# Small bf16 products on TensorE in and ahead of the router stages of a four-layer network

## The chip, the cores and the metric

The kernel runs on one core of a Trainium2 chip. The metric is the device time of one execution in microseconds (us); lower is better. TensorE's granted clock is given in the profile as a share of full speed: 1.00 is 2.4 GHz, 0.50 is 1.2 GHz.

## The reference, cut to what matters

Four layers, each an attention and then a feed-forward, over 8 x 256 = 2048 tokens of width 256. Two of the feed-forwards, those of layer 0 and of layer 3, route tokens to eight experts. The change touches only what stands at their start: the normalisation and the router's product.

```python
def _L0_ffn_ref(x, Wr, br, W_up, b_up, W_down, b_down):
    xf = x.reshape(n_tok, h)
    logits = xf @ Wr + br                     # 2048 x 256 by 256 x 8
    Sm = jax.nn.softmax(logits, axis=-1)
    G_t, idx_t = jax.lax.top_k(Sm.T, k)       # each expert takes its 256 best tokens
    ...
def _L3_ffn_ref(x, router_w, w1, w2):
    logits = x_flat @ router_w.T              # 2048 x 256 by 256 x 8
    probs = jax.nn.softmax(logits, axis=-1)
    top_v, top_i = jax.lax.top_k(probs, K)    # each token takes its 2 best experts
    ...
x = x + jnp.tanh(g_ffn[0]) * _L0_ffn_ref(_layernorm(x, axis=-1), ...)
...
x = x + jnp.tanh(g_ffn[3]) * _L3_ffn_ref(_layernorm(x, axis=-1), ...)
```

## The kernel before

Each engine has its own program, written out by hand; semaphores order them, and nothing reorders them. The stages follow each other: attention 0, feed-forward 0, attention 1, and so on. Tokens lie 128 to a tile on the partitions, in `X` (16 tiles); two tiles make a pair, so there are 8 pairs. The two feed-forwards named in `GATHERED` start like this:

- VectorE adds the last attention output to `X` (line 2238), takes the statistics (line 2014 and the short steps at lines 2020 to 2030), then normalises pair by pair into a ring of four tiles `xn` (line 2069). SyncE writes each normalised pair to memory (line 586), from where the experts' tokens are gathered later.
- TensorE waits for a pair, and turns it with four f32 transposes of 128x128 into one PSUM bank (`turn_normed`, line 828). ScalarE copies that bank to `XNT` (line 1581).
- TensorE multiplies the turned pair by the router's weights (`router`, line 836): four products a pair, each with 128 tokens as the stationary operand and the 8 columns of the router's weights as the moving one. In the profile each of these f32 products is two instructions, so a pair shows 8; a transpose is one.
- The order on TensorE is three turns, then router product and turn in alternation, and the router products of the last three pairs at the end (`layernorm`, from line 841).
- The last router product releases VectorE, which works out the softmax and the routing from the logits in `ps[0]` (from line 2477 in feed-forward 0, from line 2479 in feed-forward 3). In feed-forward 0 ten rounds of counting on VectorE and TensorE follow, in feed-forward 3 the building of slot lists; then come the experts.

The feed-forward of layer 2 uses `turn_normed` too, with no router; that of layer 1 uses it in bf16. `ident` is the f32 identity of 128x128, `ident_bf` the same in bf16. Line 1040 is the output product of an attention, the last that TensorE does before `layernorm`.

Of the kernel before, what the change touches and what calls it, by code (L numbers as in the profile page):

```python
# [8 lines left out]
BF16 = mybir.dt.bfloat16  # L9
# [66 lines left out]
LNB = 4  # L76
PAIRS = NT // ST
W2_PIECES = 4
FREE = 1
SENT0 = 16  # L80
QSTEPS = 6
# [3 lines left out]
def program(nc, a, out, stages):  # L85
    ctx = ExitStack()
    with ctx:
# [3 lines left out]
        def sb(name, shape, dt, c=ctx):  # L91
            return c.enter_context(nc.sbuf_tensor(name, shape, dt))
# [11 lines left out]
        ident = sb("ident", [P, P], F32)  # L104
        ident_bf = sb("ident_bf", [P, P], BF16)
# [194 lines left out]
        ps = [ctx.enter_context(nc.psum_tensor(f"ps{i}", [P, 2, S], F32)) for i in range(8)]  # L300
# [36 lines left out]
        GATHERED = (("ffn", 0), ("ffn", 3))  # L337
        g_order = {st: i for i, st in enumerate([st for st in stages if st in GATHERED])}

        def wait(eng, semaphore, value):  # L340

            if not isinstance(value, int) or value > 0:
                eng.wait_ge(semaphore, value)
# [55 lines left out]
        def ready_x(eng, n):  # L399

            kind, L = stages[n - 1]
            if kind == "att":
                eng.wait_ge(s["x_res"], FREE + 8 * (order["att", L] + 1))
            else:
# [21 lines left out]
        def keys_in(L, b):  # L426
            return ps[3] if L == 3 and b < 2 else P1
# [16 lines left out]
        def exists(b):  # L444
            return not isinstance(b, int) or 0 <= b < B
# [9 lines left out]
        def _(sp):  # L455
# [14 lines left out]
            def send_rows(n, b):  # L470

                rows = table[stages[n][1]]
                sp.wait_ge(s["x_res"], FREE + 8 * order["att", stages[n][1]] + b + 1)
                sp.dma_start(rows[b * S:(b + 1) * S].rearrange("(t p) c -> p t c", p=P), X[:, ST * b:ST * b + ST]).then_inc(s["rows_ready"], 16)
# [327 lines left out]
        def _(pe):  # L802
            pe.sem_inc(s["y_ps"], FREE)
            pe.wait_ge(s["ident_ready"], 3)
# [3 lines left out]
            def turn_pair(n, pair):  # L808
# [5 lines left out]
                        last = pe.transpose(turned_in(L, pair)[:, c, tt * P:(tt + 1) * P], normed_in(L, pair)[:, tt, c * P:(c + 1) * P], ident[:])  # L814
                last.then_inc(s["xnt_psum"], 1)

            def turn_normed(n, first, j):
                pair = PAIRS * n + first + j
                pe.wait_ge(s["xn_ready"], pair + 1)
                pe.wait_ge(s["xnt_done"], pair + 1)  # L820
                bank = ps[2 + j][:]
                if stages[n] == ("ffn", 1):
                    src, bank, eye = qn[j], bank.bitcast(BF16), ident_bf
                else:
                    src, eye = xn[j], ident
                for tt in range(ST):
                    for c in range(KC):
                        last = pe.transpose(bank[:, c, tt * P:(tt + 1) * P], src[:, tt, c * P:(c + 1) * P], eye[:])
                last.then_inc(s["xnt_psum"], 1)

            def router(n, pair, w):

                pe.wait_ge(s["xnt_done"], PAIRS * n + LNB + pair + 1)
                for t in range(ST * pair, ST * pair + ST):
                    for c in range(KC):
                        mm = pe.matmul(ps[0][:].rearrange("p a b -> p (a b)")[:, t * E0:(t + 1) * E0], XNT[:, c, t * P:(t + 1) * P],
                                       w[:, c], start=c == 0, stop=c == KC - 1)
                if pair == PAIRS - 1:
                    mm.then_inc(s["rt_logits"], 1)

            def layernorm(n):
                if stages[n] not in GATHERED:
                    with pe.Fori(0, PAIRS // LNB) as t:
                        for j in range(LNB):
                            turn_normed(n, LNB * t, j)
                    return

                L = stages[n][1]
                pe.wait_ge(s["rt_const"], 5)  # L850
                for pair in range(PAIRS):
                    turn_normed(n, pair - pair % LNB, pair % LNB)
                    if pair == 1:
                        pe.wait_ge(s["router"], 48 if L == 0 else 16 + 48 * (("ffn", 0) in stages))
                    if pair > 1:
                        router(n, pair - 2, wr0 if L == 0 else wr3)
                for pair in range(PAIRS - 2, PAIRS):
                    router(n, pair, wr0 if L == 0 else wr3)

            def projections(n, L):  # L860
# [4 lines left out]
                def key_product(b, par, v, f, c):  # L865
                    if (f, c) == (0, 0):
                        pe.wait_ge(ctx_sem[par], ctx_loads(i, par, v + 1))

                        if b < 4 or not keys:
                            wait(pe, k_read, 8 * i + b)  # L870
                            back = 5 if L == 1 else 4
                            if exists(b - back):
                                pe.wait_ge(s["x_res"], FREE + 8 * i + b - back + 1)
                        else:
                            pe.wait_ge(s["x_res"], FREE + 8 * i + b - 3)
                    mm = pe.matmul(keys_in(L, b)[:, f], wk[:, c, f * P:(f + 1) * P], ctxT[par][:, c], start=c == 0, stop=c == KC - 1)  # L876
# [30 lines left out]
            def attention(n, L):  # L907
# [100 lines left out]
                def output_turn(b):  # L1008
# [5 lines left out]
                    else:  # L1014
                        if exists(b + 1):
                            pe.wait_ge(s["m_lo"], 8 * m_order[L] + b + 2)
                        pe.wait_ge(s["x_res"], FREE + 8 * i + b)
                    for t in range(ST):
# [454 lines left out]
            def ffn3(n):  # L1473
# [34 lines left out]
                def down(b, k):  # L1508
# [3 lines left out]
                    for c in range(HT):  # L1512
                        if c % 2 == 0:
                            pe.wait_ge(s["f3_w2l"], W2_PIECES * t + c // 2 + 1)
                        for j, (m, w) in enumerate(((mh3, w2h_3), (mh3, w2l_3), (ml3, w2h_3))):
# [24 lines left out]
            for n, (kind, L) in enumerate(stages):  # L1540
                if kind == "att":
                    attention(n, L)
                else:
                    layernorm(n)
                    (ffn0, ffn1, ffn2, ffn3)[L](n)
# [3 lines left out]
        def _(act):  # L1549
# [252 lines left out]
            def ffn0(n):  # L1802
                route_exp(0)

                act.wait_ge(s["thr_step"], 1)
                def copy(e):
                    act.wait_ge(s["f0_xt"], e + 1)
                    wait(act, s["f0_up"], FT0 * (e - 1))
                    act.activation(xgT0[e % 2][:], ps[5][:], ACT.Copy).then_inc(s["f0_xgT"], 1)

                copy(0)
                for e in range(E0):
                    for f in range(FT0):
                        rows = P if f < FT0 - 1 else FL0
                        act.wait_ge(s["f0_up"], FT0 * e + f + 1)
                        if f == 0:
                            wait(act, s["f0_down"], e - 1)
                        act.activation(mid0[e % 2][0:rows, f], ps[f % 3][0:rows, 0], ACT.Silu,
                                       bias=bu0[0:rows, e // 2, f:f + 1]).then_inc(s["f0_mid"], 1)
                    if e + 1 < E0:  # L1820
                        copy(e + 1)
                split_k, _, middle_k, _ = splits(n + 1, 1)
                split_k(0, 0, 0)
                middle_k(0, 0)
# [86 lines left out]
            def ffn3(n):  # L1911
# [10 lines left out]
                def hidden(t, k):  # L1922
                    act.wait_ge(s["f3_up"], t + 1)
                    wait(act, s["f3_piece"], W2_PIECES * (t - 1))
                    for half in range(2):
# [5 lines left out]
                def high_w2(t):  # L1931
                    e = act.value_load(expert3_i[0:1, ds(t, 1)], min_val=0, max_val=E3 - 1)
                    act.wait_ge(s["f3_loaded"], e + 1)
                    for p in range(W2_PIECES):
                        wait(act, s["f3_piece"], W2_PIECES * (t - 1) + p + 1 if not isinstance(t, int) or t else 0)
                        act.activation(w2h_3[:, 2 * p:2 * p + 2], w2_3[:, ds(e, 1), 2 * p:2 * p + 2].squeeze(1), ACT.Copy).then_inc(s["f3_w2h"], 1)  # L1936
# [28 lines left out]
        def _(dve):  # L1965
# [591 lines left out]
            def ffn0(n):  # L2557
# [61 lines left out]
                for e in range(E0 - 3, E0):  # L2619
                    weigh(e)  # L2620
                rest_k, _, low_k, _ = rests(1)
                rest_k(0, 0)
                low_k(0, 0)
# [131 lines left out]
            def route3(n):  # L2755
# [25 lines left out]
                for j in range(2):  # L2781
                    e = dve.tensor_tensor(row_m[:, j], row_m[:, 3 + j], row_m[:, 5], ALU.mult)
                chain(e)
                running_counts(2 * E3, lambda _, e: chain(e), 0, r)
                for j in range(PAIRS3):
                    of = slice(j * E3, (j + 1) * E3)
# [50 lines left out]
            def ffn3(n):  # L2837
# [16 lines left out]
                def weigh(t, k):  # L2854
                    dve.wait_ge(s["f3_piece"], W2_PIECES * (t + 1))
                    wait(dve, s["f3_scatter"], 16 * (t - 1))
                    dve.tensor_scalar(yg3[k % 2][:], ps[5 + 2 * (k % 2)][:, 0], gate3[1][:, ds(t, 1)], None, ALU.mult).then_inc(s["f3_yg"], 1)
# [5 lines left out]
                def low_w2(t):  # L2863
                    e = dve.value_load(expert3_i[0:1, ds(t, 1)], min_val=0, max_val=E3 - 1)
                    for p in range(W2_PIECES):
                        dve.wait_ge(s["f3_w2h"], W2_PIECES * t + p + 1)
# [111 lines left out]
```

## Time and profile before

| | us |
|---|---|
| median of three executions | 1923.4 |
| the three executions | 1923.40, 1921.35, 1931.96 |
| the profiled execution, whole | 1928.71 |
| its span, first to last instruction | 1927.0 |
| TensorE matmul busy | 1578.2 (82%) |
| TensorE weight load busy | 1210.5 (63%) |
| VectorE busy | 1240.3 (64%) |
| ScalarE busy | 937.9 (49%) |

The mean granted clock of the span was 0.899. The views used are: the profile page with its 40 slices; the chain of work that ended last, in order of time; the busy time of each engine in chosen stretches, with the granted clock; and the timeline of single instructions. Durations of single matmuls on the timeline are modelled and overlap, so the distance between starts is what tells a rate.

### The profile page before, as it was taken

The page shows a single profiled execution, that of the slowest core. Times are in us where ns is not written, and L with a number is a line of the kernel's source. Part 1 is how long each engine was busy: PE and PEld are TensorE (multiplying, and loading weights), DVE is VectorE, ACT ScalarE, POOL GpSimd, SP SyncE. Part 2 cuts the span into 40 slices and gives each one's busy share as a digit, 9 for nine tenths or more (in the row PEclk, how much of TensorE's full clock was granted, in tenths as well). Part 3 has the DMA queues.
Part 4 walks back from the last instruction along what each step waited for, and adds up shares of the span by engine and source line. Part 5 has one row for each costly group of instructions (what it writes and reads, how often), then busy time and mean ns, then how long its engine had stood idle before and what let it go on. Part 6 is the DMA issues. An engine that isn't in the chain of part 4 may idle for free.

```text
span 1927.0 us, 30908 instructions
## 1 busy us (share of the span) xinstructions
PE 1578.2 (82%) x10686; PEld 1210.5 (63%) x10686; DVE 1240.3 (64%) x2750; ACT 937.9 (49%) x2051; POOL 302.5 (16%) x367
## 2 busy tenths in 40 slices
PE   5899883894788874478887999999969974899997
PEld 3566662783555543345554677788845544799997
DVE  6666628313799998766663444536359976577775
ACT  3455430322776652335554612223249961577775
POOL 2101100532121100101110000000012111234433
PEclk8899975896799987689998999999979985899999
DMA  7445234226465421435523100000167627422222
GB/s 163 60 74 84 41 118 182 45 34 123 91 131 107 76 65 47 71 46 78 73 35 161 84 1 1 0 1 1 44 83 110 103 51 262 159 38 38 41 41 28
DMA packets 86262, 144.10 MB, mean 75 GB/s; under 512 B 14031, under 2 KB 69767, under 8 KB 82937
## 3 DMA queue, kind: packets, MB, share of 16 engines
q1 hardware_dynamic: 66121, 102.76, 22.9%
q0 software_dynamic: 20016, 39.71, 12.9%
q8 instruction: 75, 1.23, 0.3%
q14 instruction: 50, 0.41, 0.1%
HBM read 75.50 MB, written 27.66 MB: 54 GB/s over the span
## 4 chain that ended last, share of the span: by engine, by line
PE 57%; DVE 24%; issue 6%; DMA 6%; ACT 5%; SPq 1%; POOL 0%; DVEq 0%; ACTq 0%; POOLq 0%
PE ps L1400 12%; PE ps L1504 7%; PE ps L1516 5%; PE ps L1369 4%; PE ps L1040 4%; DMA Qpack<-QP 3%; DVE probs L2282 3%; PE ps L987 2%; PE ps L1281 2%; PE ps L896 2%; PE ps L978 2%; PE ps L1290 2%; PE ps L926 2%; PE ps L1425 2%; PE ps L876 2%
## 5 line engine op out<-in xcount | busy, mean ns | idle before, releaser
L357 POOL DMA_DIRECT2D Kpack<-KP x192 | 101.4, 538 | 951.9 <-PE ps L1400 383.2
L1644 ACT ACTIVATE pT<-ps 128x512 f32<-128x512 f32 x256 | 151.7, 607 | 191.3 <-PE ps L981 101.9
L978 PE MATMUL ps<-Qpack,Kpack 99*128 99x256 bf16 (+1 forms) x768 | 167.1, 284 | 18.9 <-ACT pT L1649 7.4
L1504 PE MATMUL ps<-xgT,XNT 128*128 128x128 f32 x1248 | 146.4, 276 | 0.0
L1504 PEld LDWEIGHTS ps<-xgT,XNT 128*128 128x128 f32 x1248 | 143.7, 193 | 0.0
L947 PE MATMUL ps<-Kpack,Qpack 97*128 97x256 bf16 x512 | 104.4, 290 | 45.1 <-DMA Qpack<-QP 19.0
L2183 DVE CUSTOM_DVE_ANT_0 Vb<-ps,mask_bf 128x256 bf16<-128x256 f32 x256 | 95.1, 419 | 53.0 <-PE ps L947 53.0
L1649 ACT ACTIVATE pT<-ps,nmax 128x256 f32<-128x256 f32 x256 | 120.7, 531 | 12.7 <-DVE nmax L2195 12.3
L1400 PE MATMUL ps<-partB,h 128*128 128x512 f32 x512 | 121.1, 396 | 1.3 <-ACT xn L1898 1.3
L1516 PE MATMUL ps<-X_r,mh 128*128 128x256 f32 x624 | 117.7, 289 | 3.3 <-DVE X_r L2867 3.3
L1400 PE MATMUL ps<-partA,h 128*128 128x512 f32 x512 | 120.3, 395 | 0.0
L978 PEld LDWEIGHTS ps<-Qpack,Kpack 99*128 99x128 bf16 (+1 forms) x768 | 71.6, 101 | 70.3 <-ACT pT L1649 18.5
L1898 ACT ACTIVATE xn<-ps,sc 128x512 f32<-128x512 f32 x64 | 43.3, 687 | 149.0 <-PE ps L1400 149.0
L2179 DVE TENSOR_REDUCE mx<-ps 128x2 f32<-128x512 f32 x128 | 84.6, 685 | 48.3 <-PE ps L947 47.7
L987 PE MATMUL ps<-pT,V 128*32 128x256 f32 x1536 | 110.4, 403 | 4.6 <-DVE On L2215 2.3
L1400 PEld LDWEIGHTS ps<-partB,h 128*128 128x128 f32 x512 | 96.3, 188 | 23.8 <-ACT xn L1898 1.4
L1400 PEld LDWEIGHTS ps<-partA,h 128*128 128x128 f32 x512 | 96.4, 188 | 22.8 <-issue 0.5
L1658 ACT ACTIVATE probs<-ps 128x512 f32<-128x512 f32 x128 | 77.3, 615 | 64.1 <-PE ps L1072 63.7
L2867 DVE TENSOR_TENSOR X_r<-w,X_r 128x512 fp32r<-128x512 f32 x156 | 97.9, 690 | 13.4 <-ACT X_r L1936 11.8
L947 PEld LDWEIGHTS ps<-Kpack,Qpack 97*128 97x128 bf16 x512 | 43.2, 101 | 94.5 <-DVE mx L2179 28.4
L1516 PEld LDWEIGHTS ps<-X_r,mh 128*128 128x128 f32 x624 | 96.8, 191 | 3.7 <-DVE ml L2861 1.9
L2195 DVE TENSOR_REDUCE nmax<-ps 128x2 f32<-128x512 f32 x128 | 83.6, 683 | 22.5 <-PE ps L978 22.3
(323 smaller groups left out, 3654.5 us busy)
## 6 DMA issues: line engine op xcount, KB each, us to landing
Kpack<-KP POOLq DMA_DIRECT2D x192, 128.0 KB, 5.0
Qpack<-QP SPq DMA_DIRECT2D x192, 128.0 KB, 6.5
w<-in_w SPq DMA_DIRECT2D x16, 1024.0 KB, 6.0
ctxT<-in_ctxT SPq DMA_DIRECT2D x32, 256.0 KB, 7.3
h_rows<-in_h SPq DMA_DIRECT2D x16, 512.0 KB, 7.0
h<-h_rows SPq DMA_DIRECT2D x2, 4096.0 KB, 22.1
wd<-in_wd SPq DMA_DIRECT2D x4, 1536.0 KB, 14.9
xn_rows<-xn SPq DMA_DIRECT2D x16, 256.0 KB, 2.6
```

The source lines that it names most:

```text
L357: eng.dma_start(Kpack[j][DH * k:DH * (k + 1)].rearrange("d (e f) t -> d e (f t)", f=HALF), KP[par][:, part]).then_inc(done, 16)
L947: mm = pe.matmul(A[2 + h % 2][:, t], Qpack[j][0:MASK_ROW + 1, h, t * P:(t + 1) * P], Kpack[j][0:MASK_ROW + 1, h], start=True, stop=True)
L978: mm = pe.matmul(A[h % ring][:, t], Kpack[par][0:rows, h, t * P:(t + 1) * P], Qpack[par][0:rows, h], start=True, stop=L != 0)
L987: mm = pe.matmul(O[c // 2][r0:r0 + VW, c % 2], V[par][:, t, h], weights[:, t], start=t == 0, stop=t == ST - 1)
L1400: mm = pe.matmul(bank, as_read(w[:, c, o * P:(o + 1) * P], x16), as_read(part[:, v, c], x16), start=v + c == 0, stop=v == 1 and c == HT - 1)
L1504: mm = pe.matmul(bank[:, f % 4 * P:(f % 4 + 1) * P], w1_tile[k % 2][:, c, f * P:(f + 1) * P], xgT3[k % 2][:, c], start=c == 0, stop=c == K ...
L1516: mm = pe.matmul(ps[5 + 2 * (k % 2)][:, 0], m[k % 2][:, c], w[:, c], start=c + j == 0, stop=c == HT - 1 and j == 2)
L1644: act.activation(pT[h % 8][:], A[h % 2][:], ACT.Exp).then_inc(s["exp_done"], 1)
L1649: e = act.activation(pT[h][:, t], A[h % 4][:, t], ACT.Exp, bias=nmax[:, t, h:h + 1], accum_out=esum[:, t, h:h + 1])
L2179: dve.tensor_reduce(mx[:, :, h], A[2 + h % 2][:], AX.X, ALU.max).then_inc(s["smax_done"], 1)
L2183: e = dve.tensor_tensor_reduce(masked[:, 2 * (h % 2) + t], A[2 + h % 2][:, t], mask_bf[:, 0, t], 1.0, NEG_EXP, ALU.add, ALU.max, mx[:, t, ...
L2867: dve.tensor_tensor(w2l_3[:, 2 * p:2 * p + 2], w2_3[:, ds(e, 1), 2 * p:2 * p + 2].squeeze(1), w2h_3[:, 2 * p:2 * p + 2], ALU.subtract).the ...
```

## The change

A new function `filler` issues bf16 products whose result nobody reads: stationary operand `ident_bf[:, 0:32]` (32 columns), moving operand `ident` read as bf16 (256 columns), output in 32 partitions of the first half of bank `ps[7]`. One is put in front of each of the four transposes of a turn, one in front of each of the four router products of a pair, and 24 ahead of the first turn, in feed-forwards 0 and 3 alone. No wait is added, none moved, and no other engine's program changes.

```diff
+FILL, GAP_FILL = 32, 24
...
+            def filler(n, count):
+                if stages[n] in GATHERED:
+                    for _ in range(count):
+                        pe.matmul(ps[7][0:FILL, 0], ident_bf[:, 0:FILL], ident[:].bitcast(BF16), start=True, stop=True)
+
             def turn_normed(n, first, j):
...
                 for tt in range(ST):
                     for c in range(KC):
+                        filler(n, 1)
                         last = pe.transpose(bank[:, c, tt * P:(tt + 1) * P], src[:, tt, c * P:(c + 1) * P], eye[:])
...
                 for t in range(ST * pair, ST * pair + ST):
                     for c in range(KC):
+                        filler(n, 1)
                         mm = pe.matmul(ps[0][:].rearrange("p a b -> p (a b)")[:, t * E0:(t + 1) * E0], XNT[:, c, t * P:(t + 1) * P],
                                        w[:, c], start=c == 0, stop=c == KC - 1)
...
                 pe.wait_ge(s["rt_const"], 5)
+                filler(n, GAP_FILL)
                 for pair in range(PAIRS):
```

On TensorE, at the start of feed-forward 0, the rows before are these (bank and buffer numbers shown; line 1040 is the attention's output product):

```order
L1040 MATMUL ps1<-wo,OT 128x256 x4
L828 MATMUL ps2<-ident,xn0 128x128 x4
L828 MATMUL ps3<-ident,xn1 128x128 x4
L828 MATMUL ps4<-ident,xn2 128x128 x4
L836 MATMUL ps0<-wr0,XNT 128x8 x4
```

And after the change, at the same place, where lines 1049, 821, 835 and 844 are the output product, the filler, the turn and the router product:

```order
L1049 MATMUL ps1<-wo,OT 128x256 x4
L821 MATMUL ps7<-ident,ident_bf 32x256 x25
L835 MATMUL ps2<-ident,xn0 128x128
L821 MATMUL ps7<-ident,ident_bf 32x256
L835 MATMUL ps2<-ident,xn0 128x128
```

The 24 fillers of the hole and the first turn's own stand in one row; from there a filler stands before every transpose.

On TensorE, at the end of the router of feed-forward 3 before, up to the first product of the routing that follows (lines 1243 and 1244):

```order
L836 MATMUL ps0<-wr3,XNT 128x8 x4
L828 MATMUL ps5<-ident,xn3 128x128 x4
L836 MATMUL ps0<-wr3,XNT 128x8 x12
L1243 MATMUL ps2<-flags,upto 128x256
L1244 MATMUL ps2<-flags,ones_bf 128x256
```

And after:

```order
L821 MATMUL ps7<-ident,ident_bf 32x256
L844 MATMUL ps0<-wr3,XNT 128x8
L821 MATMUL ps7<-ident,ident_bf 32x256
L844 MATMUL ps0<-wr3,XNT 128x8
L1252 MATMUL ps2<-flags,upto 128x256
L1253 MATMUL ps2<-flags,ones_bf 128x256
```

Every router product now has a filler in front of it, also the twelve of the last three pairs, and nothing stands between the last router product and the routing's first. Over the kernel 176 fillers are added: for each of the two feed-forwards 24 in the hole, 32 in the turns and 32 in the router.

## Rows read from the trace of the kernel before

**Rows 1.** The page: granted clock in 40 slices, and the chain's shares by engine.

```profile
PEclk8899975896799987689998999999979985899999
PE 57%; DVE 24%; issue 6%; DMA 6%; ACT 5%; SPq 1%; POOL 0%; DVEq 0%; ACTq 0%; POOLq 0%
```

**Rows 2.** The chain, start of feed-forward 0: start us, us, what.

```profile
268.14 5.00 issue
273.14 2.79 PE ps L828 x12
...
276.92 0.49 PE ps L828 x4
277.41 0.79 PE ps L836 x8
...
281.70 0.95 PE ps L828 x4
...
285.11 4.93 PE ps L836 x24
290.24 0.30 DVE route L2477
```

**Rows 3.** The chain, start of feed-forward 3.

```profile
1585.39 4.72 issue
1590.11 2.62 PE ps L828 x12
...
1594.23 0.95 PE ps L828 x4
1595.18 1.51 PE ps L836 x8
1596.68 0.95 PE ps L828 x4
...
1610.05 0.30 DVE route L2479
```

**Rows 4.** Engines in stretches: stretch, length, busy (count) by engine, clock, DMA share, GB/s.

```profile
core 0: us, PE busy (x) PEld busy (x) DVE busy (x) ACT busy (x) POOL busy (x), PEclk, DMA share, GB/s
...
268.20:273.10 4.90, 0.00 (x0) 0.00 (x0) 3.42 (x14) 0.22 (x1) 0.00 (x0) 0.50 0.22 60
273.10:276.30 3.20, 3.16 (x16) 3.19 (x17) 2.46 (x8) 1.42 (x3) 0.00 (x0) 0.52 0.67 225
276.40:279.70 3.30, 3.30 (x32) 3.30 (x32) 2.32 (x7) 1.47 (x3) 0.00 (x0) 0.99 0.73 247
279.80:290.10 10.30, 10.22 (x50) 10.13 (x48) 0.00 (x0) 3.07 (x4) 0.00 (x0) 0.50 1.01 370
1578.00:1582.00 4.00, 2.02 (x30) 0.91 (x23) 2.26 (x7) 0.91 (x1) 0.00 (x0) 1.00 0.00 0
...
1585.40:1590.10 4.70, 0.00 (x0) 0.02 (x1) 3.48 (x14) 0.22 (x1) 0.00 (x0) 1.00 0.35 113
1590.40:1593.80 3.40, 3.40 (x19) 3.25 (x16) 2.63 (x8) 1.79 (x3) 0.00 (x0) 0.50 0.79 267
```

**Rows 5.** Timeline of TensorE in attention 0: bf16 products of 256 columns.

```profile
241.09 0.27 PE L978 MATMUL ps<-Qpack,Kpack 99*128 99x256 bf16 x1
241.20 0.27 PE L981 MATMUL ps<-mask_bf,ident_bf 128*128 128x256 bf16 x1
...
243.79 0.42 PE L981 MATMUL ps<-mask_bf,ident_bf 128*128 128x256 bf16 x1
244.00 0.42 PE L978 MATMUL ps<-Qpack,Kpack 99*128 99x256 bf16 x1
244.22 0.42 PE L981 MATMUL ps<-mask_bf,ident_bf 128*128 128x256 bf16 x1
```

**Rows 6.** Timeline of TensorE in attention 3: a bf16 pair, then f32; weight loads.

```profile
1572.17 0.39 PE L978 MATMUL ps<-Qpack,Kpack 96*128 96x256 bf16 x2
1572.40 1.03 PE L1040 MATMUL ps<-wo,On 128*128 128x256 f32 x4
...
1571.14 0.61 PEld L987 LDWEIGHTS ps<-pT,V 128*32 128x32 f32 x16 [1.47 <-DVE On L2215]
1572.17 0.11 PEld L978 LDWEIGHTS ps<-Qpack,Kpack 96*128 96x128 bf16 x2 [0.41 <-issue]
1572.30 0.73 PEld L1040 LDWEIGHTS ps<-wo,On 128*128 128x128 f32 x4
```

**Rows 7.** Timeline of VectorE, normalising in feed-forward 0.

```profile
272.31 2.78 DVE L2069 TENSOR_SCALAR xn<-X,ln_tmp 128x256 f32 x8 [0.63 <-DVE ln_tmp L2030]
```

## The prediction

> **What bounds the kernel now.** I read the page first. The chain is TensorE for 57% and VectorE for 24%, and the granted clock is far from full in some slices, among them those that hold the starts of feed-forwards 0 and 3 [rows 1]. Next the chain at those two places. In both it is one unbroken run on TensorE: an empty stretch of 5.00 us (4.72 us), filled by VectorE's statistics and first pair, then turns and router products until VectorE's first routing step is released, from 273.14 to 290.24 and from 1590.11 to 1610.05 [rows 2, 3]. The reader is to see that VectorE, ScalarE and SyncE are never named between those ends: what TensorE saves here, the end of the kernel saves, and what it spends there is paid. Last, the same stretches with their clock [rows 4]. The core enters feed-forward 0 at 0.50, is at 0.99 only from 276.4 to 279.7, and then at 0.50 until the end. In feed-forward 3 the clock is 1.00 in the hole and 0.50 from 1590.4.
>
> The price of the low clock can be read directly. A turn of four transposes takes 0.49 us fast and 0.95 us slow, a pair's router product 0.79 us and 1.51 us [rows 2, 3]. A pair therefore costs 1.28 us fast; slow, 2.45 us, the distance from the turn at 1594.23 to that at 1596.68 [rows 3]. Eight pairs are 10.2 us fast and 19.6 us slow. They took 16.9 us in feed-forward 0 (273.14 to just before 290.24, some 0.2 us of it handover) and 19.8 us in feed-forward 3.
>
> Why does the clock fall there? At 276.4 to 279.7 the weight load is busy for all of 3.30 us and the clock falls right behind it [rows 4]. So loading weights does not hold the clock; streaming columns does. In a fast pair the transposes stream for about 0.49 of 1.28 us, and a router product streams 8 columns only. The fillers put streaming there.
>
> **The change part by part.** It adds instructions on TensorE only.
>
> *A filler's own price.* bf16 products of 256 columns start 0.11 us apart at full clock and 0.215 us at half (three starts in 0.43 us) [rows 5]. A change between bf16 and f32 costs nothing more: two such products, then f32 ones start 0.23 us after the first, and the f32 weights were being loaded from 1572.30 while the second bf16 product still streamed [rows 6].
>
> *32 in the turns, in each feed-forward.* A transpose streams its own 128 columns with its load beneath it, so nothing hides the filler: 0.11 us each, a turn 0.49 + 0.44 = 0.93 us fast, and 0.95 + 0.86 = 1.81 us slow. VectorE still keeps ahead of that: eight tiles in 2.78 us is a pair every 0.70 us [rows 7].
>
> *32 in the router, in each.* A router product is bound by its two weight loads, 0.79 us for 8, so 0.10 us a load. The filler's 0.11 us of streaming can lie over the first of them. What is left is the filler's own load of 32 columns. The trace has no such row. Bounds: 0, wholly hidden, and 0.11, nothing hidden. The nearest row is line 987's load of 32 f32 columns, 16 in 0.61 us, 0.04 us each [rows 6]. I take 0.04: 0.79 + 0.16 = 0.95 us a pair fast. The Trainium skill (TensorE: Matmul & The Clock Gate, "LDWEIGHTS (loading the stationary operand)") has a load cost its columns at 1.2 GHz, which for 32 columns would be an estimated 0.027 us; by that the sum would be some 0.8 us lower. No run here shows it yet.
>
> *24 in each hole.* TensorE stands idle there for 5.00 and 4.72 us and nothing of the 24 is waited for. At half clock they take 24 x 0.215 = 5.2 us, at full clock 2.6 us, so they fit, and cost at most 0.2 us if feed-forward 0's stay slow. The turns' wait for the first pair still ends last.
>
> *What the clock gives back.* If the fillers hold it, a pair is 0.93 + 0.95 = 1.88 us, eight are 15.0 us. Feed-forward 0: 15.0 for 16.9, a gain of 1.9 us. The hole there starts at 0.50, but the fillers follow line 1040 without a break, and the clock rose after 3.2 us of unbroken work in the stretch from 273.1 [rows 4]; now that work lies in the hole. Feed-forward 3: 15.0 for 19.8, a gain of 4.8 us. There the hole is entered fast, the 24 end after 2.6 us and leave 2.1 us idle. Does the clock survive that? A stretch with TensorE busy for 2.02 of 4.00 us stayed at 1.00, the hole of 4.7 us without work was followed by 0.50 [rows 4]. 2.6 of 4.7 lies near the first, but all its idle time is in one piece, so I choose the dearer side: one slow stretch of about the 3.3 us that one lasted from 273.1, which does half its work, 1.65 us lost. Feed-forward 3 then gains 3.1 us.
>
> Sum: -1.9 - 3.1 = -5.0 us. Against the profiled execution: 1928.7 - 5.0 = 1923.7. The same shift from the median gives 1923.4 - 5.0 = 1918.4 us. Behind the two places nothing moves against the change: VectorE's routing follows at once, its inputs ready, and ScalarE has nothing on the chain there [rows 2, 3]. The 24 issue no DMA and pass no queue. The three executions before lie from 1921.35 to 1931.96, so a median of three carries some 3 us of scatter, and 0.5% (9.6 us) is about what a measurement of this kernel can tell from no change.
>
> **The rivals.**
>
> *The fillers do not hold the clock (slower).* They use 32 of the array's 128 columns. If what the chip counts is the part of the array at work, a filler counts a quarter and the low clock stays. Then each pair costs 1.81 + 1.51 + 4 x 0.08 = 3.64 us, eight 29.1 us: +12.2 and +9.3, with 0.2 in the hole +21.7, 1945.1 us; with the router's fillers wholly hidden, 26.6 us for eight, +16.7. It decides as soon as the clock is at 0.50 in the turns: there a filler costs 0.215 and brings nothing. For it: no product in these rows uses few columns alone. Against it: line 978 and line 987 stand in stretches of full clock, but neither tells the two apart. The Trainium skill (same page, "Part 4: PE-mode transpose") says that transposes do not count as work for the clock. By that the turns would rest on the fillers alone and this rival would be likelier; the trace disagrees, since from 273.1 to 276.3 there were almost only transposes and the clock rose behind them [rows 4].
>
> *The clock swings.* It holds in the turns and falls in the router-only end, or in every other stretch. Half of each: 22.05 us for eight pairs, +5.2 and +2.2, 1930.8 us. For it: in the router a filler streams 0.44 of 0.95 us, near the 2.02 of 4.00 that stayed fast, and above the 0.49 of 1.28 us that did not.
>
> *Clock held, router fillers in the open.* 0.11 instead of 0.04 on 64 of them, +4.5 us: 1922.9 us. Against it the overlap of rows 6.
>
> *All better.* Loads hidden (-2.6) and no slow stretch in feed-forward 3 (-1.65): 1914.2 us, and with scatter beyond 0.5%.
>
> **How the numbers follow.** The forecast has 0.55, the open router fillers 0.10, the swing 0.13, no hold 0.13, all better 0.09. Within 0.5% is 1913.8 to 1933.0: 0.52 of the forecast (0.03 goes to faster by scatter), 0.10, 0.11 of the swing and 0.04 of the best case make 0.77. No hold and 0.02 of the swing give slower 0.15; 0.05 of the best case and the scatter give faster 0.08. The range leaves out "no hold" and reaches from the best case less scatter, 1911, to the swing plus scatter, 1934.
>
> **What the profile would show.** Right: the clock at 1.00 from the first turn of feed-forward 0 to its last router product, a turn at 0.93 us and a router pair at 0.95 us, VectorE's first routing step at about 288.3 and 1607. Wrong clock: 0.50 in the rows of the turns, a turn of 1.8 us. Wrong price: a router pair of 1.2 us at full clock. The prediction falls if the clock behaves by something else than streaming, or if shifting the work by some microseconds changes where the clock falls in later stages, which these rows can't tell.

## The result and the profile after

The changed kernel is slower: 1981.1 us median (1975.73 to 1982.72) against 1922.4 us (1920.67 to 1931.96), a ratio of 1.0275 with a 95% interval of 1.0243 to 1.0308. The forecast was 1918.4 us, the range 1911 to 1934.

The profiled execution took 1982.42 us, 53.7 us more than that of before. From the first filler or turn to VectorE's first routing step, the two stages took 17.1 and 19.9 us before [rows 2, 3]; this is VectorE's timeline after, with what it waited for in brackets:

```profile
320.09 0.29 DVE L2486 TENSOR_TENSOR route<-ps,br 128x128 f32<-128x128 f32 x1 [34.79 <-PE ps L844]
1666.61 0.29 DVE L2488 COPY route<-ps 128x128 f32<-128x128 f32 x1 [34.72 <-PE ps L844]
```

The first turns' fillers start at 269.92 and 1615.89, so the stages now last 50.2 and 50.7 us: 33.1 and 30.8 us more. That is 10 us more than the whole kernel lost; the rest, whose code is the same but for the 24 fillers in each hole, was shorter by 3.2 us ahead of the first stage, 4.1 us between the two and 2.8 us behind the second. These parts differ by as much between kernels of this study whose code there is the same (1292 to 1304 us between the stages), so nothing is built on them.

TensorE's timeline after, the turns (line 821 the filler, line 835 the transpose, line 844 the router product); the distance between starts is what counts:

```profile
269.92 0.28 PE L821 MATMUL ps<-ident,ident_bf 128*32 128x256 bf16 x1 [2.23 <-DVE xn L2078]
270.13 0.33 PE L835 MATMUL ps<-ident,xn 128*128 128x128 f32 x1
270.39 0.28 PE L821 MATMUL ps<-ident,ident_bf 128*32 128x256 bf16 x1
...
271.97 0.40 PE L821 MATMUL ps<-ident,ident_bf 128*32 128x256 bf16 x1
272.30 0.48 PE L835 MATMUL ps<-ident,xn 128*128 128x128 f32 x1
272.70 0.40 PE L821 MATMUL ps<-ident,ident_bf 128*32 128x256 bf16 x1
...
277.84 0.40 PE L821 MATMUL ps<-ident,ident_bf 128*32 128x256 bf16 x1
278.17 0.60 PE L844 MATMUL ps<-wr,XNT 128*128 128x8 f32 x2
278.69 0.40 PE L821 MATMUL ps<-ident,ident_bf 128*32 128x256 bf16 x1
```

At full clock a filler and its transpose take 0.47 us (269.92 to 270.39), where the working had 0.11 + 0.12. At half clock they take 0.73 us, and a filler with a router product 0.85 us. 32 x (0.73 + 0.85) = 50.6 us, the whole stage. The weight loads of the same moment show why:

```profile
271.97 0.10 PEld L821 LDWEIGHTS ps<-ident,ident_bf 128*32 128x32 bf16 x1 [0.22 <-DVE xn L2078]
272.30 0.18 PEld L835 LDWEIGHTS ps<-ident,xn 128*128 128x128 f32 x1 [0.22 <-issue]
```

The transpose's load starts at 272.30, together with its own product and 0.33 us behind the filler. It was not put beneath the filler's streaming; the load engine stood idle for 0.22 us in front of it. Call this the stall. The reader compares it with the f32 load at 1572.30 before, which started while the bf16 product in front was still streaming [rows 6]. The clock, in chosen stretches (columns as in rows 4):

```profile
261.50:264.40 2.90, 2.90 (x7) 2.36 (x8) 0.00 (x0) 1.13 (x1) 0.00 (x0) 0.50 0.00 0
264.90:267.50 2.60, 2.60 (x25) 2.24 (x24) 1.97 (x7) 0.00 (x0) 0.00 (x0) 1.00 0.04 4
...
270.00:271.40 1.40, 1.40 (x7) 0.68 (x7) 1.40 (x5) 0.00 (x0) 0.00 (x0) 1.00 0.27 97
271.60:319.80 48.20, 48.20 (x154) 27.50 (x153) 3.25 (x9) 6.06 (x9) 0.00 (x0) 0.50 0.73 279
...
1616.40:1666.40 50.00, 50.00 (x159) 28.20 (x158) 4.40 (x13) 6.06 (x9) 0.00 (x0) 0.50 0.63 232
```

The first stage was entered at 1.00, where before it was 0.50 [rows 4]. The fillers did not raise the clock: it was back at 1.00 before the first of them, under the attention's output products. What they can have done is keep it through the hole. In router_only32 below, which has none there, it was at 1.00 until 276.0 and at 0.50 from 276.5, 1.4 us ahead of the first turn. Over all the profiles here, one a kernel, the clock stood at 1.00 at the first turn of feed-forward 0 in twelve of the fifteen kernels with fillers in the hole, and in none of the three without. Behind the hole the weight load is now busy for only 27.50 of 48.20 us, and the clock fell at the end of the first turn, at 271.5, and stayed down. So two things were to be told apart: the stall, and the clock.

### The profile page after: what moved, and what is told of

Read it like the earlier page. It is cut to its first block, busy times and chain, and to the rows that moved or that the text cites. A ratio compares the mean times of both kernels' runs of the same rounds, so it can differ in the third digit from the quotient of the medians.

```text
span 1980.7 us, 31260 instructions
## 1 busy us (share of the span) xinstructions
PE 1640.8 (83%) x10862; PEld 1229.5 (62%) x10862; DVE 1239.8 (63%) x2750; ACT 936.9 (47%) x2051; POOL 301.6 (15%) x367
## 3 DMA queue, kind: packets, MB, share of 16 engines
q1 hardware_dynamic: 66121, 102.76, 22.1%
q0 software_dynamic: 20016, 39.71, 12.6%
## 4 chain that ended last, share of the span: by engine, by line
PE 57%; DVE 24%; DMA 7%; issue 5%; ACT 5%; SPq 2%; POOL 0%; DVEq 0%; POOLq 0%; ACTq 0%
PE ps L1409 12%; PE ps L1513 7%; PE ps L1525 5%; PE ps L1378 4%; DVE probs L2291 3%; DMA Qpack<-QP 3%; PE ps L1049 3%; PE ps L905 2%; PE ps L996 2%; PE ps L1290 2%; PE ps L821 2%; PE ps L987 2%; PE ps L1299 2%; DVE hpart L2272 2%; PE ps L844 2%
## 5 line engine op out<-in xcount | busy, mean ns | idle before, releaser
L1658 ACT ACTIVATE pT<-ps,nmax 128x256 f32<-128x256 f32 x256 | 120.5, 530 | 13.0 <-DVE nmax L2204 12.5
```

What stands on the lines that cost most here:

```text
L1658: e = act.activation(pT[h][:, t], A[h % 4][:, t], ACT.Exp, bias=nmax[:, t, h:h + 1], accum_out=esum[:, t, h:h + 1])
```

## The experiments

All edits are to the changed kernel. The ratio is to the kernel before, run on the same chip in the same batch. "One run" is a single execution, without an interval.

| kernel | median, us | before in its batch | ratio, 95% interval | stages, us |
|---|---|---|---|---|
| fill128 | 1920.7 | 1927.0 | 0.9960 (0.9937 to 0.9983) | 17.0, 16.9 |
| hole_only | 1923.1 | 1927.0 | 0.9971 (0.9947 to 0.9996) | 19.8, 20.0 |
| grouped | 1930.5 | 1927.0 | 1.0029 (1.0002 to 1.0056) | 22.1, 22.9 |
| router_only32 | 1957.3 | 1927.0 | 1.0146 (1.0098 to 1.0194) | 35.0, 32.7 |
| router128 | 1921.5 | 1924.8 | 0.9970 (0.9949 to 0.9990) | 21.9, 13.6 |
| router128_half | 1916.7 | 1924.8 | 0.9964 (0.9937 to 0.9990) | 12.2, 12.1 |
| router128_hole36 | 1912.8 | 1924.8 | 0.9932 (0.9909 to 0.9956) | 12.6, 12.5 |
| fill32_long | 1992.1 (one run) | 1924.8 | | 40.4, 64.4 |
| fill64 | 1982.8 | 1928.2 | 1.0284 (1.0220 to 1.0348) | 47.1, 46.8 |
| fill32_f32 | 1919.1 | 1928.2 | 0.9959 (0.9933 to 0.9984) | 16.8, 16.9 |
| fill32_f32_product | 1989.5 (one run) | 1926.6 | | 47.1, 52.5 |
| fill32_bf16_turn | 1975.2 (one run) | 1926.6 | | 44.2, 43.5 |
| narrow_by_bf16 | 1935.9 (one run) | 1926.6 | | 20.2, 20.0 |
| half_hole36 | 1911.4 | 1926.6 | 0.9920 (0.9894 to 0.9947) | 12.2, 12.1 |
| fill96 | 1924.3 (one run) | 1931.1 | | 17.4, 17.5 |
| fill_rows32 | 1980.8 (one run) | 1931.1 | | 50.1, 50.6 |

### fill128: the same fillers with a full-width operand

```diff
-FILL, GAP_FILL = 32, 24
+FILL, GAP_FILL = 128, 24
```

> The changed kernel, with all 128 columns of the bf16 identity as the filler's stationary operand instead of 32. Theory A (the width): a weight load of another width than the product in flight is not put beneath it, so each change between 32 and 128 columns is paid in the open. It expects that with equal widths the load starts while the product before still streams: a turn of 4 fillers and 4 transposes near 0.93 us at full clock instead of 2.93 us, a router pair 1.2 to 1.3 us (the filler's own load of 0.10 us then lies open), eight pairs some 17.5 us, and 1918 to 1930 us in all. Theory B (the type): it is the change between bf16 and f32 that stops the loads; it expects no difference, 1981 us, a filler and a transpose still 0.73 us together.

The whole loss is gone. TensorE's timeline, turns and router at full clock:

```profile
273.19 0.27 PE L821 MATMUL ps<-ident,ident_bf 128*128 128x256 bf16 x1
273.29 0.27 PE L835 MATMUL ps<-ident,xn 128*128 128x128 f32 x1
273.40 0.27 PE L821 MATMUL ps<-ident,ident_bf 128*128 128x256 bf16 x1
...
277.73 0.27 PE L821 MATMUL ps<-ident,ident_bf 128*128 128x256 bf16 x1
277.84 0.28 PE L844 MATMUL ps<-wr,XNT 128*128 128x8 f32 x2
277.98 0.27 PE L821 MATMUL ps<-ident,ident_bf 128*128 128x256 bf16 x1
```

A filler and a transpose take 0.21 us, a filler and a router product 0.25 us: 0.86 and 1.0 us for a pair's four. That is close to what the prediction had for the 32-column filler (0.93 and 0.95 us), and less than the 1.2 to 1.3 us expected for the router pair. Theory B falls: bf16 beside f32 costs nothing. The clock had one slow stretch behind the hole, as forecast for feed-forward 3, then full speed to the end.

```profile
274.20:277.50 3.30, 3.30 (x19) 2.84 (x18) 2.21 (x7) 1.37 (x3) 0.00 (x0) 0.50 0.89 298
277.70:289.70 12.00, 12.00 (x133) 11.67 (x131) 1.44 (x4) 4.42 (x7) 0.00 (x0) 1.00 0.87 315
```

Its median is 6.3 us under the kernel before in its batch, where 5.0 us had been forecast for the narrow filler. Its profiled stages account for 3.1 us of that (17.1 and 19.9 us became 17.0 and 16.9), so the near agreement of the totals is in part luck.

### hole_only: only the 24 ahead of the stage

```diff
                 for tt in range(ST):
                     for c in range(KC):
-                        filler(n, 1)
...
                 for t in range(ST * pair, ST * pair + ST):
                     for c in range(KC):
-                        filler(n, 1)
```

> Only the 24 fillers ahead of the first turn, none in front of turns and router products. Theories A and B: all of the loss stands in the fillers between the products, so this is within 3 us of the kernel before (1919 to 1925 us); the turns of feed-forward 0 may start at full clock, worth up to 1.6 us. A third theory (C): the 24 themselves delay or slow something; it expects a loss of over 5 us.

Both stages of its profile took what the second took before, 19.8 and 20.0 us: the clock was at 1.00 in the hole and 0.50 from 274.7. So the 24 cost nothing and bring nothing by themselves; theory C falls. The median is within 0.3% of the kernel before, with an upper end of the interval just under 1; the profile shows no part that would explain a gain.

### grouped: the same 176 narrow fillers, a quarter of the changes

```diff
                     src, eye = xn[j], ident
+                filler(n, 4)
                 for tt in range(ST):
                     for c in range(KC):
-                        filler(n, 1)
...
+                filler(n, 4)
                 for t in range(ST * pair, ST * pair + ST):
                     for c in range(KC):
-                        filler(n, 1)
```

> The same 176 fillers of 32 columns, but the four of a turn stand together ahead of its four transposes, and the four of a router pair together ahead of its four products: 2 changes of width and type where the changed kernel has 8. Theories A and B, what a change costs: a quarter of the excess. If the clock holds, a pair is 0.49 + 0.44 + 0.79 + 0.44 us and about 0.4 us for the changes, 2.6 us, eight 20.5 us, 1927 us in all; if it does not, up to 4.9 us a pair and 1963 us. Theory D (each filler is dear in itself, whatever stands beside it): as the changed kernel, 1981 us.

```profile
274.96 0.66 PE L835 MATMUL ps<-ident,xn 128*128 128x128 f32 x4
275.55 0.61 PE L821 MATMUL ps<-ident,ident_bf 128*32 128x256 bf16 x4
276.09 1.06 PE L844 MATMUL ps<-wr,XNT 128*128 128x8 f32 x8
277.08 0.61 PE L821 MATMUL ps<-ident,ident_bf 128*32 128x256 bf16 x4
```

And the clock of its first stage, but for the last 2 us:

```profile
272.20:292.60 20.40, 20.40 (x154) 15.14 (x154) 4.83 (x14) 6.06 (x9) 0.00 (x0) 1.00 0.84 314
```

Four transposes take 0.59 us for 0.49 us [rows 2], a pair's router products 0.99 us for 0.79 us, four fillers 0.54 us for 0.43; a pair is 2.66 us where 2.6 us was expected, and 50 us of stage become 22. The four changes of a pair cost 0.52 us over these bare times, 0.13 us a change. Theory D falls: the price belongs to the change from one kind to the other, not to the filler.

### router_only32: narrow fillers in the router alone

```diff
                 for tt in range(ST):
                     for c in range(KC):
-                        filler(n, 1)
...
-                filler(n, GAP_FILL)
```

> Fillers of 32 columns in front of the router products alone, none in the turns, none in the hole. Theories A and B: the prices add up. A filler and a router product took 0.85 us at half clock in the changed kernel, so a pair is 3.4 us and its turn 0.95 us, eight pairs 35 us, 1955 us in all, with the clock at half. A theory by which the fillers of both kinds only hurt together (the clock) expects less than half of the loss, under 1950 us.

35.0 and 32.7 us, 1957 us: the price adds up over the changes, as expected. The first stage ran at 0.50 throughout; the second had some 3 us at 1.00.

### fill64, fill32_f32, fill32_f32_product, fill32_bf16_turn: is it the width?

fill64 takes 64 columns:

```diff
-FILL, GAP_FILL = 32, 24
+FILL, GAP_FILL = 64, 24
```

> The changed kernel with 64 columns as the filler's stationary operand. Theory A in its broad form (any width other than that of the neighbour stops the load): as the changed kernel, 0.73 us for a filler and a transpose at half clock, about 1980 us. In a narrow form (only a quarter-wide operand does it): as fill128, 0.43 us at half clock, about 1920 us.

Its timeline in the router at full clock, from one filler to the next, shows the stall; fill128 took 0.25 us for the same:

```profile
277.66 0.30 PE L821 MATMUL ps<-ident,ident_bf 128*64 128x256 bf16 x1
...
278.20 0.30 PE L821 MATMUL ps<-ident,ident_bf 128*64 128x256 bf16 x1
```

So the broad form holds so far. The clock of its first stage:

```profile
271.30:281.00 9.70, 9.70 (x44) 5.40 (x44) 4.18 (x12) 1.79 (x3) 0.00 (x0) 1.00 0.56 191
```

It stayed at 1.00 over three turns, a router pair and the next turn, stalls and all, and was at 0.50 from 281.5; the second stage did the same (1.00 from 1619.1 to 1629.0, 0.50 from 1629.5). fill32_f32 makes the filler an f32 transpose of 32 columns:

```diff
-                        pe.matmul(ps[7][0:FILL, 0], ident_bf[:, 0:FILL], ident[:].bitcast(BF16), start=True, stop=True)
+                        pe.transpose(ps[7][0:FILL, 0, 0:P], ident[:, 0:FILL], ident[:])
```

> The fillers are f32 transposes of 32 columns of the identity, of the same kind as the turn's own and with the same streaming time as the bf16 filler, so only the width changes between neighbours. Theory A: the weight load still waits, a filler and a transpose some 0.7 us at half clock, 1970 to 1990 us. If it takes width and type together to stop the load: near fill128, 1920 us.

This was a surprise: 32 columns and no stall, not even beside the router's products, which are no transposes (0.25 us from one filler to the next there, as in fill128). So width alone is not it. Two more told whether the type or the kind of operation matters. fill32_f32_product:

```diff
+                        pe.matmul(ps[7][0:FILL, 0, 0:P // 2], ident[:, 0:FILL], ident[:, 0:P // 2], start=True, stop=True)
```

> fill32_f32 took away two things at once: the type bf16, and that the filler was a matmul and not a transpose. Here the filler is an f32 matmul of 32 stationary columns (two instructions of 64 columns). If type and width together stop the load: no stall, a filler and a transpose about 0.23 us at full clock (0.43 at half), 1915 to 1930 us in all. If a narrow matmul stalls whatever its type: about 0.47 us at full clock, 1970 us or more.

fill32_bf16_turn:

```diff
+                        pe.transpose(ps[7][0:FILL].bitcast(BF16)[:, 0, 0:P], ident_bf[:, 0:FILL], ident_bf[:])
```

> The other half of the pair: the filler is a bf16 transpose of 32 columns, so it streams 128 bf16 columns, half of the changed kernel's. If type and width together stop the load: the stall is there, the filler and the transpose 0.42 us at full clock and 0.6 us or more at half, 1960 to 1985 us. If transposes are exempt: 0.17 us, under 1930 us.

TensorE's timelines, first fill32_f32 at full clock, then fill32_f32_product at full clock, then fill32_bf16_turn at half clock, each from one filler to the next with a transpose between:

```profile
278.94 0.27 PE L821 MATMUL ps<-ident 128*32 128x128 f32 x1
...
279.16 0.27 PE L821 MATMUL ps<-ident 128*32 128x128 f32 x1
```

```profile
272.48 0.30 PE L821 MATMUL ps<-ident 128*32 128x64 f32 x2
...
272.97 0.30 PE L821 MATMUL ps<-ident 128*32 128x64 f32 x2
```

```profile
273.81 0.29 PE L821 MATMUL ps<-ident_bf 128*32 128x128 bf16 x1
...
274.44 0.29 PE L821 MATMUL ps<-ident_bf 128*32 128x128 bf16 x1
```

The pair costs 0.22 us for the narrow f32 transpose and 0.49 us for the narrow f32 product, which has the same type and about the same streaming. The narrow bf16 transpose stalls too (0.63 us; its filler streams half as many columns as the changed kernel's). So neither type nor operation decides alone: of the four narrow forms only the f32 transpose is exempt.

### narrow_by_bf16: beside bf16 neighbours

```diff
             def filler(n, count):
-                if stages[n] in GATHERED:
+                if stages[n] == ("ffn", 1):
```

> The 32-column bf16 fillers stand only in front of the 32 bf16 transposes at the start of the feed-forward of layer 1 (and 24 times nowhere, since that stage has no hole fillers), beside neighbours of the same type and 128 columns. Is it the narrow bf16 load beside a wide one of any type, or beside f32 alone? If any: a filler and a transpose 0.4 us or more at full clock. If f32 alone: 0.17 us or less at full clock, 0.32 at half. In all within 5 us of the kernel before if there is no stall, some 5 to 10 us over it if there is one.

Its line picks the stage: the fillers then stand before the 32 bf16 transposes of the feed-forward of layer 1 alone.

```profile
764.53 0.40 PE L821 MATMUL ps<-ident,ident_bf 128*32 128x256 bf16 x1
764.86 0.29 PE L835 MATMUL ps<-ident_bf,qn 128*128 128x128 bf16 x1
765.08 0.40 PE L821 MATMUL ps<-ident,ident_bf 128*32 128x256 bf16 x1
```

0.55 us for the pair at half clock, with 0.22 us of idle load engine in each, as beside f32. The neighbour's type does not matter. The run was 9 us over the kernel before, as expected with a stall, but that is one execution.

### fill96 and fill_rows32: columns loaded, or part of the array?

```diff
-FILL, GAP_FILL = 32, 24
+FILL, GAP_FILL = 96, 24
```

> The changed kernel with 96 columns as the filler's stationary operand. If any number of columns other than the neighbour's 128 stops the load: as fill64, 0.49 us for a filler and a transpose at full clock, about 1980 us. If what counts is that the operand takes a smaller part of the array (a tile of 32 or 64, which 96 is not): as fill128, 0.22 us, about 1920 us.

fill_rows32 keeps `FILL` at 32 and narrows the partitions, not the columns:

```diff
-                        pe.matmul(ps[7][0:FILL, 0], ident_bf[:, 0:FILL], ident[:].bitcast(BF16), start=True, stop=True)
+                        pe.matmul(ps[7][:, 0], ident_bf[0:FILL, :], ident[0:FILL].bitcast(BF16), start=True, stop=True)
```

> The filler's operands have 32 partitions instead of 128, and the stationary one all 128 columns. If what counts is the number of columns loaded: no stall, about 1920 us. If it is the part of the array that is addressed, rows like columns: the stall is there, 0.47 us for a filler and a transpose at full clock, about 1980 us.

fill96, at half clock, from one filler to the next with the transpose between:

```profile
272.05 0.42 PE L821 MATMUL ps<-ident,ident_bf 128*96 128x256 bf16 x1
...
272.48 0.42 PE L821 MATMUL ps<-ident,ident_bf 128*96 128x256 bf16 x1
```

fill_rows32, at full clock:

```profile
272.28 0.28 PE L821 MATMUL ps<-ident,ident_bf 32*128 32x256 bf16 x1 [2.23 <-DVE xn L2078]
272.49 0.33 PE L835 MATMUL ps<-ident,xn 128*128 128x128 f32 x1
272.75 0.28 PE L821 MATMUL ps<-ident,ident_bf 32*128 32x256 bf16 x1
```

### fill32_long: the stall and the clock apart

Each filler streams its 256 columns twice, so 512, and the hole has 12 of them:

```diff
-FILL, GAP_FILL = 32, 24
+FILL, GAP_FILL = 32, 12
...
-                        pe.matmul(ps[7][0:FILL, 0], ident_bf[:, 0:FILL], ident[:].bitcast(BF16), start=True, stop=True)
+                        pe.matmul(ps[7][0:FILL], ident_bf[:, 0:FILL], ident[:].bitcast(BF16).unsqueeze(1).to_broadcast([P, 2, S]), start=True, stop=True)
```

> The changed kernel with fillers of 32 columns that stream 512 columns instead of 256 (12 in the hole): the stalls of the changes of width stay, but the share of the time in which columns stream goes up. If the second half of the loss was the clock, it stays at full here: a filler and a transpose 0.47 + 0.11 = 0.58 us, a filler and a router product about 0.65 us, eight pairs 39 us a stage and about 1965 us in all. If the clock is at half for another reason, a filler and a transpose take 0.95 us and it is over 2000 us.

```profile
272.00:305.00 33.00, 32.97 (x133) 16.17 (x133) 4.96 (x14) 5.69 (x9) 0.00 (x0) 1.00 0.74 287
1616.00:1677.00 61.00, 61.00 (x154) 27.52 (x153) 2.94 (x8) 6.07 (x9) 0.00 (x0) 0.50 0.52 195
```

The first stage came out as expected: full clock up to 309, 0.58 us a filler and transpose, 40 us in all. The second fell to half clock at its start and never rose, 64 us, so the total of 1965 us was missed. In this one execution, then, longer streaming held a full clock over the stalls, but did not bring back a lost one through them.

### The other side: where the gain is

router128 keeps 128-column fillers in the hole and the router, router128_half has one for every second router product, router128_hole36 has 36 in the hole; half_hole36 is the last two together, and it is its edit that is shown.

```diff
-FILL, GAP_FILL = 32, 24
+FILL, GAP_FILL = 128, 36
...
                 for tt in range(ST):
                     for c in range(KC):
-                        filler(n, 1)
...
                 for t in range(ST * pair, ST * pair + ST):
                     for c in range(KC):
-                        filler(n, 1)
+                        filler(n, 1 - c)
```

> Fillers of 128 columns, in front of the router products and 24 in the hole, none in the turns. In fill128 a turn with fillers took 0.87 us and a router pair 1.0 us at full clock, and no stall was left. Theory A: the turn goes back to 0.49 us, a pair is 1.49 us, eight 11.9 us where fill128 took 16.8 and 16.7 us; if the clock holds through both stages that is 5 us less in each, 10 us under fill128, about 0.8% under the kernel before. A rival: without fillers in the turns the clock falls again, a pair is then near 0.95 + 1.6 us and the gain is gone, within 0.3% of the kernel before.

> As router128, but one filler in front of every second router product. If the clock holds: 0.49 + 0.89 us a pair, eight 11.0 us, some 1.5 us under router128 in all. If half the fillers are too few for the clock: the stages at half clock after the first pairs, within 0.3% of the kernel before.

> As router128, with 36 fillers in the hole instead of 24: at full clock they last 4.0 of the hole's 4.7 to 5.0 us, so the clock should not fall in it. Against router128: up to 1.6 us less in each stage where router128 falls behind the hole; if the hole is entered at half clock, 36 take up to 7.7 us and the first turn comes up to 2.7 us late.

> The two parts that helped put together: 128 columns, 36 in the hole, none in the turns, one filler in front of every second router product. The turn stays at 0.47 us, a router pair is 0.95 us instead of router128_hole36's 1.0 us: 0.4 us less a stage if the clock holds, so within 1 us of it, about 1912 us. If every second is too few for the clock in some executions, it is between router128_half and router128_hole36, 1912 to 1917 us.

router128's two stages took 21.9 and 13.6 us with the same code. Its stretches, then those of router128_hole36 (the first stage, the hole ahead of the second, the second):

```profile
271.20:273.70 2.50, 0.55 (x4) 0.42 (x4) 1.59 (x5) 0.22 (x1) 0.00 (x0) 1.00 0.36 112
274.50:294.80 20.30, 20.24 (x121) 19.81 (x120) 3.52 (x10) 5.50 (x9) 0.00 (x0) 0.50 0.91 339
1599.00:1612.00 13.00, 13.00 (x127) 12.88 (x127) 4.69 (x14) 6.06 (x9) 0.00 (x0) 0.88 0.90 320
```

```profile
273.70:286.10 12.40, 12.24 (x128) 11.63 (x128) 4.88 (x14) 6.06 (x9) 0.00 (x0) 1.00 0.76 253
1580.70:1585.50 4.80, 4.08 (x37) 3.41 (x35) 3.41 (x14) 0.21 (x1) 0.00 (x0) 1.00 0.34 111
1585.50:1597.80 12.30, 12.17 (x128) 11.64 (x128) 4.92 (x14) 6.06 (x9) 0.00 (x0) 1.00 0.84 288
```

With 24 fillers the hole keeps over 2 us of idle time, and in router128 the clock fell behind it in both stages. In the second it fell as the turns began, at 1598.8, and was back at 1602.2, behind twelve transposes in a row and the first two router products. In the first it fell 1.3 us into the turns, at 274.4, and did not come back in the 20 us that followed, in which turns and router products alternate. So the router's fillers held a full clock in one stage and did not bring a lost one back in the other. That fits its spread, 1912.2 to 1929.8 us, and a median some 11 us over what was expected, but one execution was profiled, and the kernel before spreads from 1919.9 to 1933.4 us in the same batch. With 36 both stages ran at 1.00 throughout, 12.6 and 12.5 us, and the spread is 1908.5 to 1916.2. router128_half, with 24 in the hole, had both stages at 1.00 in its profile too, 12.2 and 12.1 us where 11.0 was expected, yet its runs spread the most, from 1903.8 to 1932.2 us; no profile shows where its slow ones lose. half_hole36 has 12.2 and 12.1 us, 1911.4 us, a ratio of 0.9920 (0.9894 to 0.9947), with an interval wholly under 1: some 15 us under the kernel before and 70 under the changed one. Whether it beats router128_hole36 can't be told; their intervals overlap.

## Why the prediction was wrong

- **What bounds the kernel.** Right. The two stages lie on the chain alone, and what they gained or lost reached the end in every profiled execution, to within the 12 us by which the rest of the kernel differed.
- **Why the clock falls.** Right in kind. Fillers with enough streaming held it (fill128, grouped, router128_hole36). Against the rival that a 32-column filler counts a quarter speaks grouped, whose narrow fillers held 1.00 through most of its first stage.
- **24 in the hole.** Right: no cost. The slow stretch chosen for feed-forward 3 came in fill128's two stages, once each. That the fillers of feed-forward 0 would raise the clock was not what happened here: it had risen without them.
- **A filler's own price.** This is the step that failed: "A change between bf16 and f32 costs nothing more" was true and answered the wrong question. Rows 6 compare instructions that both use the whole array. The filler differs in type and in the part of the array it addresses, and only the first was priced. The bound of the router's filler, "0 and 0.11", was no bound either: it excluded that the filler could delay its neighbours. Measured, the two changes around a filler cost 0.25 us beside a transpose (0.47 for 0.22) and 0.30 us beside a router product (0.54 to 0.55 in fill64 for 0.25), at full clock. A turn that was to take 0.93 us took 4 x 0.47 = 1.88 us at full clock, and a router pair 4 x 0.55 = 2.2 us instead of 0.95. 32 x 0.55 = 17.6 us of stalls a stage, where the whole expected gain was 1.9 and 3.1 us.
- **What that did to the clock.** The clock fell although there were fillers everywhere. That the stalls brought this about, by taking the streaming's share away, is argued and not shown: fill128 without stalls kept its clock but for one stretch, and fill32_long with longer streaming held it in its first stage; but fill64, with the same stalls, held 1.00 for 10 us in each stage, while the changed kernel fell in the first turn. The sizes add up: a stage of 15 us as forecast, 17.6 us of stalls at full clock, and the rest to 50.2 and 50.7 us, some 18 us, because nearly all of it ran at half.
- **The rivals.** "The fillers do not hold the clock" gave the sign and a half of the symptom, a turn at half clock, but priced it at 1.81 us; it was 4 x 0.73 = 2.92 us. Its 21.7 us were 53.7.

The trace of before did hold a row for it. In attention 0 a product of 32 columns follows one of 128, on TensorE's timeline:

```profile
241.54 0.27 PE L978 MATMUL ps<-Qpack,Kpack 99*128 99x256 bf16 x1
241.65 0.27 PE L981 MATMUL ps<-mask_bf,ident_bf 128*128 128x256 bf16 x1
241.85 0.54 PE L987 MATMUL ps<-pT,V 128*32 128x256 f32 x4
```

Starts 0.11 us apart, and then 0.20 us, at the one place where `128*128` becomes `128*32`. The same 0.20 us stands in front of line 987 at 247.28, 253.35 and 256.71, and no wait is named there. Line 987 had been read for its load time alone.

## What to carry to other kernels

Price an added TensorE instruction together with its neighbours: look in the trace for the same change of the shape in front of and behind it, since an operand of 32 or 64 columns, or of 32 rows, between full-array ones cost 0.25 to 0.30 us in stalled loads at full clock here, however short its own load, unless it was an f32 transpose. Filler work for the clock should use all 128 columns, should stand where the streaming is thin and nowhere else, and should leave little idle time in front of the stage (0.75 us with 36 in router128_hole36); then it paid 0.8% here. Narrow products that are needed are best issued in runs, as line 987 is.

## What the runs showed of the hardware that was not expected

- A filler of 32 or 64 columns, or of 32 partitions, put 0.25 to 0.27 us on a filler-and-transpose pair at full clock, and the ones of 32 columns or partitions 0.30 us at half; 96 columns put none.
- An f32 transpose of 32 columns was exempt (0.22 us for the pair), a bf16 transpose and an f32 product of 32 columns were not.
- The same code took 21.9 and 13.6 us in the two stages of one execution (router128). In both the clock fell at or soon behind the hole; in one it was back 3.4 us later, in the other it stayed at 0.50 to the end of the stage.
